# A modulated 1-D convolution network on one core: where the split of Q3 for a later group stands, and where VectorE's edge operations stand

## The reference, cut to what matters

```python
def _layer(x, style, w, b, mw, mb, typ):
    s = style @ mw.T + mb
    weight = SCALE * w * s[:, None, :, None]
    demod = lax.rsqrt(jnp.sum(weight * weight, axis=(2, 3)) + EPS)
    weight = weight * demod[:, :, None, None]
    blur_k = jnp.asarray(BLUR_K)
    if typ == 'same':
        out = jax.vmap(_conv_same)(x, weight) + b[None, :, None]
    elif typ == 'upsample':
        out = jax.vmap(_conv_up)(x, weight.transpose(0, 2, 1, 3)) + b[None, :, None]
        out = _blur(out, 2.0 * blur_k, (1, 1))
    elif typ == 'downsample':
        xb = _blur(x, blur_k, (2, 2))
        out = jax.vmap(_conv_down)(xb, weight) + b[None, :, None]
    return out
# TYPES = ('same', 'upsample', 'same', 'downsample')
return x + four layers of x, each with its own weights
```

## Time and profile before

| | us |
|---|---|
| median of 3 runs (822.36 to 827.84) | 827.11 |
| the profiled execution | 828.73 |
| its span, first to last instruction | 826.9 |
| TensorE busy in it | 706.6 |
| VectorE, GpSimd, ScalarE busy | 448.2, 390.9, 312.8 |

### The profile page before, as it was taken

How to read it: one execution, slowest core, us unless ns; L and a number is a source line. 1 busy time by engine, 2 the same in 40 slices (tenths; PEclk the granted TensorE clock), 3 DMA queues, 4 the chain that set the end, 5 groups by cost and what they waited for, 6 DMA issues and landing times.

```text
span 826.9 us, 12320 instructions
## 1 busy us (share of the span) xinstructions
PE 706.6 (85%) x4434; PEld 652.0 (79%) x4434; DVE 448.2 (54%) x711; ACT 312.8 (38%) x501; POOL 390.9 (47%) x520
## 2 busy tenths in 40 slices
PE   4586999878889999897789999987978999999986
PEld 4576888868878888896779888886968888888876
DVE  6959645555445455465455545445544455555560
ACT  4223344333334444433343444333343444444341
POOL 3552455543545545444444555553445544555430
PEclk9879899989889999998898999999989999999998
DMA  5043656575545767573557665756634776767653
GB/s 205 17 105 71 160 144 158 133 148 121 143 122 132 172 173 172 121 173 104 120 122 172 147 169 146 168 113 137 156 115 109 173 173 150 163 154 172 165 138 119
DMA packets 130092, 116.98 MB, mean 141 GB/s; under 512 B 6064, under 2 KB 96560, under 8 KB 130032
## 3 DMA queue, kind: packets, MB, share of 16 engines
q1 hardware_dynamic: 129376, 114.62, 58.3%
q10 hardware_dynamic: 656, 1.57, 0.6%
HBM read 36.47 MB, written 33.55 MB: 85 GB/s over the span
## 4 chain that ended last, share of the span: by engine, by line
PE 68%; POOL 11%; DVE 10%; issue 6%; ACT 3%; DMA 1%; POOLq 0%; ACTq 0%; DVEq 0%; SPq 0%
PE po L170 12%; PE po L171 12%; PE po L172 12%; PE pg L170 7%; PE pg L172 6%; PE pg L171 6%; PE pg L176 3%; PE pg L175 3%; POOL Gl L601 3%; POOL Gh L179 3%; POOL Q3l L582 3%; POOL Q3h L179 3%; DVE Gf L701 2%; ACT Gh L482 2%; PE pm L172 1%
## 5 line engine op out<-in xcount | busy, mean ns | idle before, releaser
L170 PE MATMUL po<-xh,W 128*128 128x256 f32 (+1 forms) x640 | 229.1, 358 | 5.4 <-issue 5.4
L171 PE MATMUL po<-xl,W 128*128 128x256 f32 (+1 forms) x640 | 227.4, 355 | 0.0
L172 PE MATMUL po<-xh,W 128*128 128x256 f32 (+1 forms) x640 | 224.8, 351 | 0.0
L170 PEld LDWEIGHTS po<-xh,W 128*128 128x128 f32 x640 | 132.8, 208 | 17.7 <-issue 5.6
L598 POOL TENSOR_TENSOR Gl<-Gf,Gh 128x512 fp32r<-128x512 f32 x31 | 47.6, 1536 | 208.6 <-ACT Gh L482 208.6
L172 PEld LDWEIGHTS po<-xh,W 128*128 128x128 f32 x640 | 131.8, 206 | 15.3
L171 PEld LDWEIGHTS po<-xl,W 128*128 128x128 f32 x640 | 132.2, 207 | 11.7
L590 POOL TENSOR_TENSOR Q2l<-Q2f,Q2h 128x512 fp32r<-128x512 f32 x31 | 72.8, 2350 | 68.8 <-ACT Q2h L477 68.8
L482 ACT CAST Gh<-Gf 128x512 fp32r<-128x512 f32 x64 | 39.7, 621 | 167.0 <-DVE Gf L701 167.0
L705 DVE TENSOR_TENSOR Wf<-pg,S 128x512 f32<-128x512 f32 x64 | 44.1, 691 | 108.1 <-PE pg L172 89.2
L170 PE MATMUL pg<-Q3h,A2h 128*128 128x256 f32 x64 | 24.8, 387 | 86.3 <-POOL Q3h L179 84.7
(11 more groups left out here) (175 smaller groups left out, 1693.0 us busy)
## 6 DMA issues: line engine op xcount, KB each, us to landing
X<-in_xin SPq DMA_DIRECT2D x64, 516.0 KB, 4.7
out<-T SPq DMA_DIRECT2D x64, 512.0 KB, 3.1
W<-W SPq DMA_DIRECT2D x96, 256.0 KB, 5.9
W<-W SPq DMA_DIRECT2D x32, 384.0 KB, 6.7
V<-V SPq DMA_DIRECT2D x32, 128.0 KB, 5.3
V<-W SPq DMA_DIRECT2D x32, 64.0 KB, 3.9
V<-Vx SPq DMA_DIRECT2D x32, 64.0 KB, 3.8
E<-in_ed ACTq DMA_DIRECT2D x1, 768.0 KB, 8.0
```

Source lines behind the costliest of these rows:

```text
L170: eng.matmul(o, wh_, rh, start=first, stop=False)
L171: eng.matmul(o, wh_, rl, start=False, stop=False)
L172: return eng.matmul(o, wl_, rh, start=False, stop=last)
```

## The change

Three loops are edited; no instruction is added, removed or resized. On ScalarE `q3_high(g + 3)` moves from the end of the fourth sample to the end of the second. On GpSimd `q3_full(g + 3)` moves from the third to the second sample, ahead of `x_parts`, and `q3_low(g + 3)` from the fourth to the second, between `x_parts` and `finish`. VectorE's edge operations move by one sample: from the end of the third to the end of the fourth (in group 0 from each sample to the next).

```diff
@@ scalar
-                if i == 3 and g + 3 < NGR:
+                if i == 1 and g + 3 < NGR:
                     q3_high(g + 3)
@@ gpsimd
+                if i == 1 and g + 3 < NGR:
+                    q3_full(g + 3)
                 if i == 1 and g + 1 < NGR:
                     x_parts(b // Q + 3)
-                if i == 2 and g + 3 < NGR:
-                    q3_full(g + 3)
-                if i == 3 and g + 3 < NGR:
+                if i == 1 and g + 3 < NGR:
                     q3_low(g + 3)
                 if b % Q == 1 and b > Q:
                     finish(b // Q - 1)
@@ vector
-                if (g, i) in edge_at:
-                    c, k = edge_at[g, i]
+                if divmod(b - 1, NG) in edge_at:
+                    c, k = edge_at[divmod(b - 1, NG)]
                     edge(c, k)
```

## The result

| | before | after |
|---|---|---|
| median, us | 827.19 (822.36 to 827.84, 4 runs) | 908.45 (902.80 to 912.48, 4 runs) |
| ratio to before | | 1.099, 95% interval 1.092 to 1.106 |
| profiled execution, its span, us | 828.73, 826.9 | 902.80, 901.0 |
| mean granted clock in it | 0.926 | 0.851 |

What follows compares the result with a forecast made beforehand. Bound after the change: the W loop, TensorE's conv waiting each group for W copies behind a late store on SyncE. 86.1 + 1.5 + 28 × 27.2 + 59.1 + 2.5 = 910.8, plus 1.8: 912 us; 8-in-10 range 848 to 945.

Steps and rivals of the forecast that it cites:

- The Q3 waits go; W's copies take their place: TensorE's 29 waits for Q3's low part, 84.7 us, go; a wait of about 5 us for W precedes each group's conv.
- Edges later cost nothing in the 12 groups: VectorE's moved edge lists delay only the fourth sample's output and Q2f, which has until the third sample: no cost.
- Term 1 to 4: From conv start C through casts of Vx and Q3, Q3's low parts and finish to the store: C + 12.1 us.
- Term 5: On SyncE's queue, from issue of the store to the landing of the last W copy: 12.4 us.
- Term 6: From the landing of the last W copy to the start of TensorE's conv: 0.2 us.
- The lost clock, 2.5 us: TensorE's clock at half speed after each wait for W lengthens the loop by 2.2 to 2.8 us, taken as 2.5.
- The sign that I gave: In the profile after the change, TensorE's mean granted clock falls below 0.926.
- Group 0, net 1.5 us later at group 1's first conv: TensorE waits some 8 us for VectorE's second edge list, less the gone Q3 wait: net 1.5 us, between −4 and 5.
- The end, 59.1 + 2.5 us: From group 29's first conv on: 59.1 us as before, plus 2.5 us for a slow start at group 29.
- B: Rival: same loop through W's copies, but TensorE's clock stays up; 24.7 us a group, 840 us; chance 0.08.
- C: Rival: W no bound, its copies at 373 GB/s; 767 us, or about 722 at TensorE's own work; chance 0.10.
- D: Rival: VectorE's later edge list makes conv wait for Q2f and output; up to 4.7 us in 12 groups; chance 0.06.

Runs made afterwards that it cites:

- the eighth experiment: Changed kernel with ScalarE's cast of Q3 at the head of the second sample's list from group 1 on, ahead of W's cast: 804.51 us, ratio 0.975.
- the fifth experiment: Changed kernel with unit 1 of groups 4 to 29 computed 19 times instead of once, to keep TensorE busy through the wait: 862.05 us, ratio 1.039.
- the first experiment: Changed kernel with VectorE's edge operations back in their old place, so only Q3 stands earlier: 894.64 us, ratio 1.081.
- the fastest kernel: Changed kernel with finish ahead of Q3's low parts, SyncE's copies ahead of store and load, and group 0's edges back: 698.26 us, ratio 0.842.

## Why the prediction was right

Step by step, the forecast's terms and what the profile and the runs showed.

- *The Q3 waits go; W's copies take their place.* Right, by the waits after, and by the experiment that changed only SyncE's order in the changed kernel and was 204 us faster than it.
- *Edges later cost nothing in the 12 groups.* Right in this kernel, 26.97 against 26.95 us a group, but not for the reason given. Alone they bring 3.5%, which the W loop hides. It hides a cost too: `Q2f` did not have until the third sample, because GpSimd splits it at the first sample, ahead of all else that leads to `finish`. That pushes the store by 3.6 us in groups 5, 13 and 21 of the eighth experiment, and puts VectorE's `T` within 0.7 to 1.0 us of holding the conv in the same groups here.
- *Term 1 to 4, the store at C + 12.1 at full clock.* Right: 12.2 to 12.4 us in the groups of the fifth experiment in which the clock stayed up, all but one of them (group 5, 14.0 us, behind the longest edge list).
- *Term 5, 12.4 us from store to landing.* The 28 groups show 11.5 to 13.8, mean 12.3.
- *Term 6, 0.2 us.* Mean 0.21.
- *The lost clock, 2.5 us.* The mean store at C + 14.5 less 12.2 makes 2.3 us. The sign that I gave, a mean clock under 0.926, came too, but is a poor measure: the first experiment has the same period at a mean of 0.889.
- *The group, 27.2 us.* 26.95, which takes 7 us off the sum.
- *Group 0, net 1.5 us later at group 1's first conv.* Undersized; the range given, to 5, held it. It was 4.7 us later, 90.86 against 86.13. The waits moved as forecast. After the change:

```profile
75.18 3.57 PE L371 MATMUL pe<-U,E 128*128 128x320 f32 x6 [7.85 <-DVE U L758]
...
87.52 1.65 PE L374 MATMUL pe<-b1s,E 128*128 128x128 f32 x6 [2.26 <-DVE b1s L770]
```

Before it:

```profile
67.64 1.88 PE L371 MATMUL pe<-U,E 128*128 128x320 f32 x6 [0.49 <-DVE U L758]
...
77.40 1.04 PE L374 MATMUL pe<-b1s,E 128*128 128x128 f32 x6 [2.00 <-DVE b1s L770]
...
83.86 0.55 PE L170 MATMUL pg<-Q3h,A2h 128*128 128x256 f32 x1 [5.42 <-POOL Q3h L179]
```

The wait for the second list grew by 7.4 us, that for the third by 0.3, and Q3's 5.4 us went: 2.2 us more idle time from the first conv of group 0 to that of group 1. What I left out is the clock: TensorE was busy 29.6 us in that stretch and 27.2 before, 2.4 us more for the same work. The edge products behind the first wait show it, 3.57 against 1.88 us.
- *The end, 59.1 + 2.5 us.* Oversized: from 845.48 to 901.0 it took 55.5 us, 6.1 less. Group 29 took 19.65 us, only 0.3 more than before: I added 2.5 us for a slow start, which it had before the change too (a clock of 0.81 over its first 6 us, 0.74 now). The last group but one took 18.33 us and not 21.04, since its W copies came 2.4 us earlier after its conv (874.76 − 865.13 against 799.11 − 787.09). The last took 1.2 us less, because its clock stayed up behind a wait of 2.6 us, where it had been 0.75 behind one of 5.4.

The misses of 3 us up, 7 and 6 us down lead from the sum, which is 912.6, to the profiled 902.8. That was the fastest of the four runs. The median is 908.45; no trace shows where the 5.6 us between them lie, so that the forecast comes within 4 us of the median is in part luck.

Of the rivals, B (the clock stays up) is what the fifth experiment built, at 862 us rather than 840, with added work in 26 groups and the clock not up in all of them. C (W no bound) came out only where the order was changed: 704.82 us, near the 722 that I gave for a kernel bound by TensorE's work. The rate of the copies was 194 to 207 GB/s in the stretches read in three kernels, so the 373 GB/s on which C rested was not seen for them. The Trainium skill (DMA: Bandwidth & Descriptors, "Where 436 GB/s comes from") names 435 GB/s for transfers within SBUF; no trace comes near it for these copies. D (the edges decide) fell with the first experiment, as far as this kernel goes.

## What to carry to other kernels

Where an instruction moves up in a list, ask not only who waited for it, but who stands behind its new place and what that one, in turn, holds back in another queue: here it was a four-number copy on GpSimd, behind it a store, and behind the store the weights. A wait in an in-order queue delays everything behind it, so put the transfer on which the next stage depends ahead of one that nobody needs soon; it gave 22% here. When a wait goes, look up by how much the next arrival was in time, on the group where it was latest: 0.9 us of slack cannot take 4.6 us of delay.

## What the runs showed that I had not expected

More work made the kernel faster: 936 added matmuls brought 46 us, since TensorE's clock, which fell to half at each of the 28 waits in the changed kernel, stayed at full speed at 23 of the 26 convs ahead of which the work was put.

VectorE and GpSimd slow each other in much of their work. In the eighth experiment the same sum `Vf` took 0.56 us in all 15 groups in which GpSimd did nothing beside it, and up to 1.35 us beside a busy one (start, duration):

```profile
456.61 0.56 DVE L726 TENSOR_TENSOR Vf<-Wf 128x384 f32<-128x384 f32 x1
...
476.14 1.34 DVE L726 TENSOR_TENSOR Vf<-Wf 128x384 f32<-128x384 f32 x1
```

GpSimd's four-number copy of `finish` took 0.80 us there, against 0.19. In the fastest kernel VectorE is busy 511.6 us with the instructions that took 448.2 before. The Trainium skill (GPSIMD Engine Reference, "Specifications") says that the two share SBUF interfaces and contend where a VectorE instruction has two SBUF inputs, as this sum has; these rows agree. It isn't always VectorE that pays: in the trace of before `Vf` started at 794.37 and took 0.56 us, and the row of `x_parts` that started 0.08 us behind it took 1.44 us, against a median of 1.10. A kernel made denser pays this back in part, and the next gain would have to reckon with it.
